# One transformer layer on one core: projections of a group interleaved with attention of the group ahead, transposes by DMA inside SBUF

## The chip, the cores and the metric

The kernel runs on one NeuronCore of one Trainium2 chip. The number that counts is the device time of one execution in microseconds. A core has five engines that run side by side: TensorE (PE in the profile; its weight loads are PEld), VectorE (DVE), ScalarE (ACT), GpSimd (POOL) and SyncE (SP), whose queue here issues every DMA. They meet only at semaphores.

## What is computed

The input x is 4 batches of 2048 rows of 512 numbers in fp32. The reference, cut to what matters:

```python
h = layernorm(x)
q, k, v = relu(h @ Wq + bq), relu(h @ Wk + bk), relu(h @ Wv + bv)
e = q @ k.T / sqrt(512)          # causal: later keys are masked
y = softmax(e) @ v               # per batch
x = x + layernorm(relu(y @ Wo + bo))
h2 = layernorm(x)
# for two scores (so, si): grouped convolution of h2 (4 columns to 1),
# batch norm over all 8192 rows, gelu, linear, softmax
out = (h2 @ W) * top32(softmax(so)) + (h2 * top32(softmax(si))) @ W + bias
x = x + layernorm(out)
```

The batch norm needs the mean and variance over all rows of all batches. So there are two phases: the first (layer norm, attention, residual, the convolution and its statistics) has to end before the second (gelu, linear, top 32, the output) may begin.

## The kernel before

A tile is 128 rows, so a batch has 16 tiles, and a group is 4 tiles (512 rows). Every fp32 operand of a large product is split into two fp16 halves, hi and lo, and `three` (L445 to L450) issues three matmuls for each product: hi by hi, hi by lo, lo by hi. A full step is 4 slices of 128 in the contraction by 3, which is 12 matmuls of 128x512.

The first phase (L342 to L941) is a hardware loop over the 4 batches (`Fori`), one body for each engine. What PE does in the body, in this order, is `pe_steps` (L217 to L231):

- For each of the 4 groups: 4 steps each of v, k and q (a step is 128 of the 512 output channels), in which the tiles of the next group are transposed (`hT`), and then 4 steps `vo`, which multiply v by Wo ahead of the attention. This part of the body is called projections below.
- Then, for i from 0 to 17 (`attention_steps`, L200): the scores of tile i against all keys up to it (`s`, one step for each chunk of 512 keys), and for tile u = i-2 the product of the softmax with v (`pv`), chunk by chunk. Ahead of the product of a chunk stands the transposition of the next (`pT`). In the last i of a batch the first four tiles of the next batch are transposed as well.

A transposition is done by PE. It takes an fp32 tile in SBUF, multiplies it by the identity (L475, L527) into one of two PSUM banks (`T_BANK`), from which ACT takes the hi half (`hi_half`, L563, with the instruction in L567) and DVE the lo half (`lo_half`, L681, with L685). PE may use the bank again when DVE has read it: `take_t` waits on `t_lo` of two transpositions back (L454). The product of a chunk waits on `t_lo` of its own (L535).

Other banks: 4 (`M_BANK`) for projections, scores and the transposed convolution, 2 (`Y_BANK`) for the products. `take_m` (L457) waits until the step four places back has been read out.

ACT reads each v, k, q step twice (L582 into `raw`, L583 into the hi half), DVE subtracts (L708). ACT takes exp (L658), bias and norm work on the attention output follow on ACT (L592, L597), DVE (L721, L727, L729, L734, L736, L743) and POOL (L894 to L910). DVE does the convolution as a product and a reduction, twice for each tile (L750, L753), PE transposes its result (`conv_transposes`, L464, instruction L467), ACT adds the channel bias (L606), DVE takes the statistics (L759). All three steps of a tile lag its attention by some i.

SBUF: one area `work` of 7168 words serves the transposed input, the input itself, the scores and the transposed softmax in turn, because projections and attention don't overlap. SP issues the loads and stores in order; its plain loads of x go to `work`.

The second phase (L948 to L1400) is a loop over groups of 8 tiles, and the change doesn't touch it but for the view of `bn_all` that L1253 reads.

## Time and profile before

| | |
|---|---|
| median of 3 runs | 2333.42 us (2332.57 to 2333.52) |
| profiled execution | 2331.11 us |
| its span | 2329.3 us |
| PE, DVE, ACT, POOL busy | 90%, 69%, 52%, 39% |
| DMA engines, queue of SP | 19.7% of 16 engines |
| granted clock of TensorE | 0.976 on the mean |

The span is what lies between the first and the last instruction that the profiler recorded, the time is that of the whole execution. PE's line in 40 slices shows the two phases: nines and eights up to slice 27 (about 1570 us), a slice with two tenths, and eights beside a DVE and a POOL at nine after it. Matmuls are pipelined: one of 128x512 is shown with 379 ns, but the next one starts earlier than that, so the busy time of PE is more than the time it needs.

### The profile page before, as it was taken

Reading aid. Unit: us, or ns where it says so; the run is one execution under the profiler, and the core shown is the slowest. Engines: PE = TensorE matmul, PEld = TensorE weight load, DVE = VectorE, ACT = ScalarE, POOL = GpSimd, SP = SyncE. Lnnn points to the kernel's source line nnn. Section 1 sums busy time; section 2 is a strip of 40 time slices with the busy share of each in tenths; the row PEclk is TensorE's granted clock in tenths of the full one; section 3 lists DMA queues with packets and bytes.
Section 4 is the critical chain, followed back from the end, with each engine's and each line's share of the span. In section 5 each row is a group of like instructions: output and inputs, shape, how many; then the busy total and the mean of one; then the engine's idle time right before and its main releaser. Section 6 shows DMA issues by size and latency. Waiting matters only on the chain. (4 is left out here: it accounts for less than half of the span.)

```text
span 2329.3 us, 37816 instructions
## 1 busy us (share of the span) xinstructions
PE 2088.6 (90%) x10313; PEld 1019.8 (44%) x10313; DVE 1596.3 (69%) x3574; ACT 1203.9 (52%) x2483; POOL 906.0 (39%) x1127
## 2 busy tenths in 40 slices
PE   5999999999999899999999999964888887888985
PEld 2444454444455444545444445532333333433432
DVE  6544756543665655376655357577999999999994
ACT  4443323444332344333244433234888888888886
POOL 1101212100221200021210022124999999999998
PEclk9999999999999999999999999996999999999998
DMA  4101212100211200021211012122222222222232
GB/s 146 53 10 39 80 48 76 56 26 7 71 64 48 86 30 33 26 77 62 69 49 42 8 55 80 48 89 96 88 89 84 84 86 90 77 88 89 77 96 76
DMA packets 91008, 151.19 MB, mean 65 GB/s; under 512 B 9538, under 2 KB 27074, under 8 KB 90820
## 3 DMA queue, kind: packets, MB, share of 16 engines
q1 hardware_dynamic: 90820, 149.05, 19.7%
q8 instruction: 73, 1.20, 0.2%
q14 instruction: 115, 0.94, 0.2%
HBM read 86.10 MB, written 62.91 MB: 64 GB/s over the span
## 5 line engine op out<-in xcount | busy, mean ns | idle before, releaser
L448 PE MATMUL psum<-work,w_hi 128*128 128x512 f16 x1536 | 457.9, 380 | 7.3 <-DVE w_lo L678 3.7
L448 PE MATMUL psum<-v,work 128*128 128x512 f16 x1632 | 374.4, 379 | 35.2 <-DVE work L685 35.1
L567 ACT ACTIVATE work<-psum 128x512 f16<-128x512 f32 (+2 forms) x228 | 125.3, 551 | 496.9 <-PE psum L527 462.4
L448 PE MATMUL psum<-kT,qT 128*128 128x512 f16 (+3 forms) x1920 | 364.3, 348 | 0.0
L448 PE MATMUL psum<-work,w_lo 128*128 128x512 f16 x768 | 291.6, 380 | 0.0
L685 DVE SCALAR_TENSOR_TENSOR work<-psum,work 128x512 f16<-128x512 f32 (+2 forms) x228 | 144.1, 632 | 181.2 <-ACT work L567 179.2
L448 PEld LDWEIGHTS psum<-kT,qT 128*128 128x128 f16 x1920 | 181.4, 98 | 168.8 <-issue 2.0
L582 ACT ACTIVATE work<-psum,bqkv_s 128x512 f32<-128x512 f32 x192 | 132.1, 688 | 236.4 <-PE psum L448 233.7
L448 PEld LDWEIGHTS psum<-v,work 128*128 128x128 f16 x1632 | 156.7, 98 | 212.3 <-DVE work L685 48.7
L1292 DVE MAX8 c<-cut 128x8 f32<-128x512 f32 x384 | 244.1, 675 | 4.6 <-DVE cut L1288 4.6
L448 PEld LDWEIGHTS psum<-work,w_hi 128*128 128x128 f16 x1536 | 150.2, 98 | 178.5 <-issue 5.2
L908 POOL TENSOR_SCALAR ve<-mv 128x1 f32<-128x1 f32 x66 | 14.6, 221 | 536.8 <-DVE mv L736 536.8
L894 POOL TENSOR_SCALAR ve<-mv 128x1 f32<-128x1 f32 x65 | 15.8, 244 | 488.9 <-DVE mv L729 485.2
L1076 PE MATMUL psum<-fw,xsT 128*128 128x512 f16 x792 | 197.7, 403 | 1.1 <-ACT xsT L1178 1.1
L1076 PE MATMUL psum<-fw,h2T 128*128 128x512 f16 x780 | 179.3, 379 | 0.0
L1288 DVE MATCH_REPLACE8 cut<-c,cut 128x512 f32<-128x512 f32 x256 | 170.7, 673 | 0.0
L448 PE MATMUL psum<-w_hi,vT 128*128 128x512 f16 x512 | 154.9, 379 | 0.0
L904 POOL TENSOR_TENSOR xr<-ob,xr 128x512 f32<-128x512 f32 x66 | 83.5, 1265 | 146.0 <-ACT ob L597 146.0
L708 DVE TENSOR_TENSOR qT<-work,qT 128x512 f16<-128x512 f32 x64 | 44.3, 692 | 115.6 <-ACT qT L583 115.6
L1076 PEld LDWEIGHTS psum<-fw,xsT 128*128 128x128 f16 x792 | 82.1, 104 | 92.2 <-issue 20.5
L448 PEld LDWEIGHTS psum<-work,w_lo 128*128 128x128 f16 x768 | 75.3, 98 | 91.1 <-issue 0.8
L1076 PEld LDWEIGHTS psum<-fw,h2T 128*128 128x128 f16 x780 | 76.5, 98 | 77.9 <-issue 0.5
(140 smaller groups left out, 3880.1 us busy)
## 6 DMA issues: line engine op xcount, KB each, us to landing
work<-x SPq DMA_DIRECT2D x72, 256.0 KB, 3.2
out<-zn SPq DMA_DIRECT2D x70, 256.0 KB, 3.0
h_scratch<-hb SPq DMA_DIRECT2D x68, 256.0 KB, 3.1
x_scratch<-xr SPq DMA_DIRECT2D x66, 256.0 KB, 2.9
x<-x_scratch SPq DMA_DIRECT2D x66, 256.0 KB, 2.8
h<-h_scratch SPq DMA_DIRECT2D x65, 256.0 KB, 3.7
xr<-x SPq DMA_DIRECT2D x64, 256.0 KB, 2.9
xc_scratch<-xcT SPq DMA_DIRECT2D x68, 128.0 KB, 1.7
```

Of the source, the lines that this page charges most:

```text
L448: mm = nc.tensor.matmul(outp, stat(a), mov(c), start=(n == 0 and k == 0), stop=(n == total - 1 and k == 2))
L567: nc.scalar.activation(dst, src, ACT.Copy, scale=scale).then_inc(t_hi.sem, 1)
L582: nc.scalar.activation(raw[:, n % 2, :], bank, ACT.Relu, bias=bias, scale=QKV_DOWN)
L685: nc.vector.scalar_tensor_tensor(dst, src, scale, hi, ALU.mult, ALU.subtract).then_inc(t_lo.sem, 1)
L708: nc.vector.tensor_tensor(dst[:, 1], raw[:, n % 2, :], dst[:, 0], ALU.subtract).then_inc(vkq_lo.sem, 1)
L894: nc.gpsimd.tensor_scalar(ve2[:], m[:, 1:2], EPS * O_GAIN * O_GAIN, None, ALU.add).then_inc(ve2_ok.sem, 1)
L904: nc.gpsimd.tensor_tensor(xr[:, t % 4, :], ob[:, t % 2, :], xr[:, t % 4, :], ALU.add).then_inc(x1_ok.sem, 1)
L908: nc.gpsimd.tensor_scalar(ve3[:], mv3[:, t % 2, 1:2], EPS, None, ALU.add).then_inc(ve3_ok.sem, 1)
L1076: mm = nc.tensor.matmul(outp, stat(a), mov(c), start=(fresh and n == 0 and k == 0), stop=(n == total - 1 and k == 2))
L1288: nc.vector.match_replace(dst, eight, src, 0.0).then_inc(top_ok.sem, 1)
L1292: nc.vector.max(dst, src).then_inc(top_ok.sem, 1)
```

## The change

The first phase is written anew. The second stays, and so does the arithmetic: the same products in the same halves.

- **Order.** The 16 groups of all batches go through one unrolled program (no `Fori` in the first phase). Time is counted in halves H, eight for each group g. PE's list for a half is `pe_items(H)`: two projection steps of group g (v in halves 0 and 1, q in 2 and 3, k in 4 and 5, vo in 6 and 7), and one piece of attention of group g-1 (scores of its tiles 1, 2, 3 in halves 0, 2, 4, products of its tiles 0 to 3 in halves 1, 3, 5, 6) or, in half 7, the scores of tile 0 of g itself. The later work on a tile (bias, norms, residual, convolution) is given out by `due(H, lag)`. After the last group there are 12 more halves without projections.
- **Transpositions.** `hT` and `pT` on PE are gone (L475, L527). ACT and DVE or POOL make the two fp16 halves in SBUF in the natural layout (`hhl`, `phl`), and SP transposes each half with a DMA from SBUF to SBUF (`dma_start_transpose`). The hi half of the input comes from ACT (`hi_h`), its lo half now from POOL (`lo_h`), those of the softmax from ACT (`hi_p`) and DVE (`lo_p`). The two small transpositions of the convolution stay on PE.
- **Banks.** The two banks of transpositions join the others, so `M_BANK` has 6.
- **Buffers.** The shared `work` area is replaced by buffers of their own: input 4 tiles, its halves 4 tiles, transposed input 2 groups, scores 2 tiles (before 3), softmax halves 4 chunks, transposed softmax 4 chunks (before 2). qT holds two groups in place of a batch.
- **Queues.** SP runs through stores, loads and DMA transposes in one order written out by half. A transpose of chunk n waits for its lo half and for the product of chunk n-4.
- **Start.** The identity, the biases and the mask are loaded behind the weights and the first transposes; PE waits for all five of them before its first matmul. The priming of semaphores and of buffers by zeros, which the loop needed, goes.

The core of the diff:

```diff
+def stages(H):
+    g, h = divmod(H, HALF)
+    kind, c = (VQK + ("vo",))[h // 2], 2 * (h % 2)
+    return [(kind, g, c), (kind, g, c + 1)] if g < NG else []
+def s_tile(H):
+    g, h = divmod(H, HALF)
+    if h == 7 and g < NG:
+        return GROUP * g
+    if h in (0, 2, 4) and 0 < g <= NG:
+        return GROUP * (g - 1) + 1 + h // 2
+    return None
+def pv_tile(H):
+    g, h = divmod(H, HALF)
+    if h in (1, 3, 5, 6) and 0 < g <= NG:
+        return GROUP * (g - 1) + (1, 3, 5, 6).index(h)
+    return None
+def due(H, lag):
+    g, h = divmod(H - lag, HALF)
+    if h in (2, 3, 5, 6) and 0 < g <= NG:
+        return GROUP * (g - 1) + (2, 3, 5, 6).index(h)
+    return None
+def pe_items(H):
+    attention = []
+    if s_tile(H) is not None:
+        attention = [("s", s_tile(H), j) for j in range(chunks(s_tile(H)))]
+    if pv_tile(H) is not None:
+        attention = [("pv", pv_tile(H), j) for j in range(chunks(pv_tile(H)))]
+    items = stages(H) + attention if H % HALF < 2 else attention + stages(H)
+    if due(H, 4) is not None:
+        items.append(("x", due(H, 4)))
...
@@ -92,8 +173,7 @@
-        T_BANK = [psum[:, n, :] for n in (0, 1)]
-        M_BANK = [psum[:, n, :] for n in (2, 3, 4, 5)]
+        M_BANK = [psum[:, n, :] for n in range(6)]
         Y_BANK = [psum[:, n, :] for n in (6, 7)]
 
...
@@ -110,19 +190,17 @@
-            qT = sa("qT", [P, 2, C, S], F16)
+            qT = sa("qT", [P, 2, 2, C, 512], F16)
             kT = sa("kT", [P, 2, C, S], F16)
             v = sa("v", [P, 2, TILES, D], F16)
-            work = sa("work", [P, 7168], F32)
-            hT = [work[:, 2048 * n:2048 * (n + 1)].bitcast(F16).rearrange("p (h c n) -> p h c n", h=2, c=C)
-                  for n in (2, 0)]
-            xg = work[:, 2048:4096].rearrange("p (j n) -> p j n", j=GROUP)
-            raw = work[:, 6144:7168].rearrange("p (s n) -> p s n", s=2)
-            sS = [work[:, 2048 * n:2048 * (n + 1)] for n in range(3)]
-            pT = work[:, 6144:7168].bitcast(F16).rearrange("p (s h n) -> p s h n", s=2, h=2)
             vT = sa("vT", [P, 2, C, 512], F16)
+            hT = sa("hT", [P, 2, 2, C, 512], F16)
+            xg = sa("xg", [P, GROUP, D], F32)
+            hhl = sa("hhl", [P, GROUP, 2, D], F16)
+            raw = sa("raw", [P, 2, D], F32)
+            sS = sa("sS", [P, 2, S], F32)
+            phl = sa("phl", [P, 4, 2, 512], F16)
+            pT = sa("pT", [P, 4, 2, 512], F16)
...
@@ -338,109 +358,104 @@
+                def transpose_h(g, j):
+                    need(sp, vqk_ps, vqk_at("k", g - 2, C - 1))
+                    sp.wait_ge(h_lo.sem, h_lo.at(GROUP * g + j))
+                    for a in range(2):
+                        sp.dma_start_transpose(hT[:, g % 2, a, :, P * j:P * (j + 1)], hhl[:, j, a, :]).then_inc(hT_in[j].sem, 16)
+                def transpose_p(T):
+                    for j in range(chunks(T)):
+                        n, w = chunk_at(T, j), width(T, j)
+                        need(sp, pv_ps, n - 4)
+                        sp.wait_ge(p_lo.sem, p_lo.at(n))
+                        for a in range(2):
+                            sp.dma_start_transpose(pT[:, n % 4, a, 0:w].rearrange("p (c n) -> p c n", n=P), phl[:, n % 4, a, 0:w]) \
+                                .then_inc(pT_in[n % 4].sem, 16)
...
+                for H in range(HALVES):
+                    g, h = divmod(H, HALF)
+                    if h == 3 and pv_tile(H) is not None:
+                        transpose_p(GROUP * (g - 1) + 2)
+                    if h == 5 and pv_tile(H) is not None:
+                        transpose_p(GROUP * (g - 1) + 3)
+                    rows_of(H)
+                    if h == 1 and pv_tile(H) is not None:
+                        transpose_p(GROUP * (g - 1) + 1)
+                    if h == 4 and g + 1 < NG:
+                        transpose_h(g + 1, 0)
+                        transpose_h(g + 1, 1)
+                    if h == 5 and g + 2 < NG:
+                        for j in range(GROUP):
+                            load_x(g + 2, j)
+                    if h == 6 and g + 1 < NG:
+                        transpose_h(g + 1, 2)
+                        transpose_h(g + 1, 3)
+                    if h == 7 and g < NG:
+                        transpose_p(GROUP * g)
...
@@ -449,497 +464,467 @@
+                def take_m(item):
+                    n = m_place[item]
+                    if n >= 6:
+                        signal, i = m_freed(m_items[n - 6])
+                        pe.wait_ge(signal.sem, signal.at(i))
+                    return m_bank(item)
...
+                def product(T, j):
+                    n, t = chunk_at(T, j), T % TILES
+                    if j == 0:
+                        pe.wait_ge(vo_lo.sem, vo_lo.at(T))
+                        need(pe, o_ev, T - 2)
+                    pe.wait_ge(pT_in[n % 4].sem, pT_in[n % 4].at(n // 4))
+                    for k in range(width(T, j) // P):
+                        mm = three(Y_BANK[T % 2], GROUP * j + k, t + 1, lambda a: pT[:, n % 4, a, P * k:P * (k + 1)],
+                                   lambda a: v[:, a, GROUP * j + k, :])
+                    mm.then_inc(pv_ps.sem, 1)
...
+                def hi_h(g, j):
+                    act.wait_ge(hn_ok.sem, hn_ok.at(GROUP * g + j))
+                    need(act, hT_in[j], g - 1)
+                    nc.scalar.activation(hhl[:, j, 0, :], xg[:, j, :], ACT.Copy).then_inc(h_hi.sem, 1)
...
+                def hi_p(T, part):
+                    for j in range(chunks(T))[part]:
+                        n, w = chunk_at(T, j), width(T, j)
+                        act.wait_ge(p_ok.sem, p_ok.at(T))
+                        need(act, pT_in[n % 4], n // 4 - 1)
+                        nc.scalar.activation(phl[:, n % 4, 0, 0:w], sS[:, T % 2, 512 * j:512 * j + w], ACT.Copy, scale=P_SCALE) \
+                            .then_inc(p_hi.sem, 1)
...
-                def lo_half(b, step, dst, hi, scale):
-                    dve.wait_ge(t_hi.sem, t_at(t_hi, b, step))
-                    src = t_bank(step)[:, 0:dst.shape[-1]] if len(dst.shape) == 2 else t_bank(step).rearrange("p (c n) -> p c n", c=C)
-                    nc.vector.scalar_tensor_tensor(dst, src, scale, hi, ALU.mult, ALU.subtract).then_inc(t_lo.sem, 1)
...
+                def lo_p(T, part):
+                    for j in range(chunks(T))[part]:
+                        n, w = chunk_at(T, j), width(T, j)
+                        dve.wait_ge(p_hi.sem, p_hi.at(n))
+                        nc.vector.scalar_tensor_tensor(phl[:, n % 4, 1, 0:w], sS[:, T % 2, 512 * j:512 * j + w], P_SCALE,
+                                                       phl[:, n % 4, 0, 0:w], ALU.mult, ALU.subtract).then_inc(p_lo.sem, 1)
...
+                    if h == 0:
+                        if st:
+                            lo_vqk(*st[0])
+                        late(H, (5, conv_stats), (2, residual_stats))
+                        if st:
+                            lo_vqk(*st[1])
+                        if s is not None:
+                            score_rows(s)
+                        late(H, (3, convolution))
+                    elif h == 1:
+                        early = s_tile(H - 1)
+                        for n, part in ((0, first), (1, rest_of)):
+                            if st:
+                                lo_vqk(*st[n])
+                            if early is not None:
+                                lo_p(early, part)
+                        late(H, (3, convolution))
+                        if g + 1 < NG:
+                            ln_stats(g + 1, 2)
+                            ln_stats(g + 1, 3)
+                    elif h == 2:
+                        if s is not None:
+                            score_rows(s)
...
+                def lo_h(g, j):
+                    pool.wait_ge(h_hi.sem, h_hi.at(GROUP * g + j))
+                    nc.gpsimd.tensor_tensor(hhl[:, j, 1, :], xg[:, j, :], hhl[:, j, 0, :], ALU.subtract).then_inc(h_lo.sem, 1)
```

## Rows read from the trace of the kernel before

**Rows 1.** Busy time by stage: stretch, its length, each engine, granted clock, DMA share, GB/s
```profile
27.60:1558.00 1530.40, 1481.43 (x7549) 745.25 (x7550) 877.44 (x1887) 588.40 (x1054) 227.42 (x412) 1.00 0.15 51
1558.00:1583.00 25.00, 2.97 (x13) 1.38 (x11) 18.04 (x37) 6.16 (x15) 7.60 (x14) 0.60 0.32 110
1583.00:2329.30 746.30, 600.05 (x2737) 270.17 (x2737) 684.91 (x1631) 600.69 (x1407) 663.94 (x684) 0.94 0.28 86
```

**Rows 2.** Timeline of PE in the attention of the last batch: start, length, instructions
```profile
1485.41 9.88 PE L448 MATMUL psum<-kT,qT 128*128 128x512 f16 x48
1495.13 0.60 PE L527 MATMUL psum<-idn,work 128*128 128x128 f32 x4
1495.57 2.75 PE L448 MATMUL psum<-v,work 128*128 128x512 f16 x12
1498.16 0.60 PE L527 MATMUL psum<-idn,work 128*128 128x128 f32 x4
1498.60 2.75 PE L448 MATMUL psum<-v,work 128*128 128x512 f16 x12
```

**Rows 3.** Transpositions on PE, groups by shape: count, busy us, mean ns, idle before
```profile
L527 PE MATMUL psum<-idn,work 128*128 128x128 f32 x544 | 86.2, 274 | 10.2 <-DVE work L685 6.7 <-ACT work L658 3.4
L475 PE MATMUL psum<-idn,work 128*128 128x128 f32 x272 | 42.6, 282 | 19.7 <-DVE work L701 16.9 <-DVEq L796 2.8
L467 PE MATMUL psum<-idn,xcs 128*128 128x128 f32 x132 | 25.7, 277 | 9.3 <-ACT xcT L606 9.3
```

**Rows 4.** What PE's weight loads waited for, 27.6 to 1558 us: us, times, longest
```profile
PEld psum L448 <- DVE work L685: 53.0, 38, 2.8
PEld psum L527 <- DVE work L685: 8.7, 8, 1.9
```

**Rows 5.** DMA: the queue of SP (packets, MB, share), two issues (KB, us to landing)
```profile
q1 hardware_dynamic: 90820, 149.05, 19.7%
xc_scratch<-xcT SPq DMA_DIRECT2D x68, 128.0 KB, 1.7
bqkv_s<-bqkv SPq DMA_DIRECT2D x1, 6.0 KB, 1.6
```

**Rows 6.** Timeline of SP: one issue
```profile
1530.12 0.33 SPq L386 DMA_DIRECT2D xc_scratch<-xcT  x1
```

**Rows 7.** Groups by shape of the engines beside PE, first phase: count, busy us, mean ns
```profile
L582 ACT ACTIVATE work<-psum,bqkv_s 128x512 f32<-128x512 f32 x192 | 132.1, 688 | 236.4 <-PE psum L448 233.7 <-DVE w_lo L678 2.0 <-DVE kT L708 0.7
L567 ACT ACTIVATE work<-psum 128x512 f16<-128x512 f32 x180 | 106.9, 596 | 402.7 <-PE psum L527 368.2 <-PE psum L475 34.1
L685 DVE SCALAR_TENSOR_TENSOR work<-psum,work 128x512 f16<-128x512 f32 x180 | 123.8, 688 | 150.6 <-ACT work L567 148.5 <-ACTq L624 1.8
L835 DVE TENSOR_SCALAR_CACHE_REDUCE work<-psum 128x512 f32<-128x512 f32 x96 | 63.8, 690 | 29.9 <-PE psum L448 28.9
L658 ACT ACTIVATE work<-work,nm 128x2048 f32<-128x2048 f32 x4 | 8.0, 1993 | 0.0
L743 DVE TENSOR_SCALAR hb<-xr,mv,rs 128x512 f32<-128x512 f32 x66 | 38.2, 579 | 0.6 <-POOL rs L910 0.6
L750 DVE TENSOR_TENSOR prod<-hb,cw_b 128x512 f32<-128x512 f32 x131 | 90.3, 690 | 6.4
L753 DVE TENSOR_REDUCE xcs<-prod 128x128 f32<-128x512 f32 x131 | 89.9, 686 | 5.2
L904 POOL TENSOR_TENSOR xr<-ob,xr 128x512 f32<-128x512 f32 x66 | 83.5, 1265 | 146.0 <-ACT ob L597 146.0
```

**Rows 8.** Timeline at the start: layer norm's statistics, its scaling, PE's first product
```profile
9.18 0.18 DVE L696 BATCH_NORM_AGGREGATE mv<-st 128x2 f32<-128x6 f32 x1
...
27.60 1.01 PE L448 MATMUL psum<-work,w_hi 128*128 128x512 f16 x2 [3.70 <-DVE w_lo L678]
```

**Rows 9.** Timeline between the phases: last product, last statistics, second phase's first
```profile
1555.13 2.75 PE L448 MATMUL psum<-v,work 128*128 128x512 f16 x12
...
1583.56 3.64 DVE L1253 BATCH_NORM_AGGREGATE bn_mv<-bn_all 128x2 f32<-128x384 f32 x2 [1.99 <-PEq L342]
```

More of the change, by code:

```diff
@@ L81, in sem, with sig @@
             return ctx.enter_context(nc.semaphore(name))
[L83 to L84 removed]
+        def sig(name, step=1):
+            return Count(sem(name), step)
         x1_d = nc.dram_tensor("x1_scratch", [(B + 1) * TILES + GROUP, P, D], F32, kind="Internal").ap()
@@ new lines, in conv_stats, with late @@
+                def conv_stats(T):
+                    for r in range(2):
+                        wait_apart(dve, x_ev, x_ev.at(T))
+                        i = nc.vector.bn_stats(bn_all[:, T, r, :], xcT[:, T % 2, r, :])
+                    i.then_inc(bn_ok.sem, 1)
+                def late(H, *steps):
+                    for lag, step in steps:
+                        if due(H, lag) is not None:
+                            step(due(H, lag))
+                for j in range(GROUP):
+                    ln_stats(0, j)
```

1006 lines of the change are left out of this document (421 added, 585 removed).

## The prediction

> **What bounds the kernel now.** I read the stages first. The span falls into a start (27.6 us), the first phase up to PE's last product (1530.4), a drain (1558 to 1583.6) and the second phase (745.7) [rows 1, 9]. The second phase isn't touched: its DVE and POOL instructions stay, so its 745.7 us go into the sum unchanged. In the first phase PE shows 1481 of 1530 us at full granted clock, DVE 877, ACT 588, POOL 227 [rows 1]; PE is the bound. How much of that is needed, the busy time doesn't tell, since a matmul's shown length overlaps the next. The timeline does: 12 matmuls of 128x512 begin at 1495.57 and what follows them at 1498.16, so one costs 0.216 us of stream; four transpositions begin there and the next product at 1498.60, so one costs 0.11 [rows 2]. The scores of three full chunks and one of 384 take 9.72 us, which leaves 0.162 for a 384 wide one [rows 2]: cost goes by columns.
>
> From the loops, a batch has 768 projection matmuls, 336 of full score chunks, 408 of products: 1512 x 0.216 = 326.6 us. Narrow chunks are 48 each of 384, 256 and 128 columns, 48 x 0.324 = 15.6. Four batches make 1368.6 us. Transpositions of inputs and softmax: 544 + 272, less 16 before the first product, are 800 x 0.11 = 88 us; those of the convolution 126 x 0.11 = 13.9 [rows 3]. 1530.4 - 1368.6 - 88 - 13.9 leaves 60 us in which PE stood still. The waits name them: its weight loads waited 53.0 + 8.7 = 61.7 us for the lo half of a transposition by DVE [rows 4]. So the transpositions cost 88 us of stream and about 60 of waiting.
>
> **The change, part by part.**
>
> Transpositions off PE: minus 88 us, on the path, as PE is the bound. The convolution's stay, 13.9.
>
> The waits: minus 60, and new ones come. What a product now waits for is a longer chain, but it has a longer lead. Chain after a tile's last score matmul: eviction 0.69, maximum about 0.1, exp up to 1.99, hi half about 0.6, lo half 0.69, two DMA transposes [rows 7], taking the durations of the nearest forms; both halves read SBUF now, which I price the same. That is 4.1 us without the DMAs. Shortest lead, tile 1 in a group with one chunk a tile: two projection steps (5.2), a product, the next scores, two more steps, about 13 us. On the way stand, in DVE's order, a convolution (0.58 + 2 x (0.69 + 0.69) = 3.3 us) and the lo half of the next projection step [rows 7]; so some 9 us plus DMAs against 13. In groups of four chunks the lead is over 20 us for tiles 0 to 2; for tile 3 the transposes wait for the products of tile 2 chunk by chunk (four buffers), so the first pair has two chunks' matmuls of 2.6 us each and the two steps between, some 12 us, and then a pair every 2.6 us.
>
> The six banks: a step waits for the one six places back, 6 x 2.6 = 15.6 us at PE's pace, against 0.69 x 2 of ACT behind an exp of 1.99. I cost it at nothing; ACT's own order covers it.
>
> Other engines: DVE loses the input's lo half (64 x 0.688 = 44 us), ACT's count stays, POOL gains 64 x 1.265 = 81 us [rows 7]. DVE 877 - 44 = 833 of some 1410 us, ACT 588, POOL 308: none is a bound on the mean. By group it is closer. One with attention of one-chunk tiles gives PE 41.5 us of projections (192 x 0.216) and 10 blocks of 128x128 keys at 1.3 (12 narrow and 3 wide matmuls): 54 us. DVE has 16 lo halves (11 us), four tiles of later work at about 6.4, input statistics and scaling 6, scores and softmax halves 6: 48 to 49. So DVE is at nine tenths there, in four groups of 16. I put 2 us into each.
>
> The DMA transposes: 128 for inputs and 320 for softmax chunks. Counted in blocks of 128x128 that is 512 + 1088 = 1600, so 400 full ones of 128x512 fp16 (128 KB). They go through one queue in order. PE leaves 1412 / 400 = 3.5 us for each. In a group with four-chunk tiles there are 148 blocks, 37 full ones, in 41.5 + 58 x 1.3 = 117 us: 3.2 us each. The trace has no such DMA. From below: a plain one of 128 KB is issued in 0.33 us and lands after 1.7 [rows 5, 6]. From above: the queue's 90820 packets took 19.7% of 16 engines over 2329.3 us, which is 81 ns each at 1.6 KB [rows 5]. A transpose can't move rows of 1 KB whole. Cut at the 128 columns of a block it has 512 packets, 512 / 16 x 81 ns = 2.6 us; cut into half that, 5.2 us, and finer still 10. A packet of little content should cost less than 81 ns: the bias load, 128 runs of 48 bytes, lands in 1.6 us like the large one [rows 5]. I take 2.2 us, between 1.7 and 2.6, the ends nearest to a row. At 2.2 the queue is used for 880 of 1412 us and the transposes are hidden, but the tight leads above (9 us plus a pair of 4.4 us against 13) are used up. I put 30 us of stalls into the sum (0 to 60): 8 for DVE, 12 for eight groups with short tiles at 1.5 us, 10 for the fourth tiles and the last group, whose attention no projections cover.
>
> Here two rules of the Trainium skill stand against each other, and the trace can't decide. "Advanced Engine Details and Errata", section on the X-bar transpose, says that transpose DMAs on this chip are as fast as regular ones: then the sum holds with stalls near 0. "VectorE: DVE Perf Modes", section on the three transpose paths, lists 1309 ns for a 128x128 block by DMA. Taken as time for each of four blocks one after the other, that is an estimate of 5.2 us for a full one, and the kernel would take about 2890 us.
>
> Start: statistics end at 9.18 before [rows 8]; then scaling, hi halves, POOL's four lo halves (5.1 us), eight transposes behind 4 MB of weights, and five constants behind those, for which PE now waits. I get 27 to 34 us for the first product, and take 30 (27.6 before).
>
> Drain: from the last product the last tile goes through bias, relu, statistics, scale, norm, residual, statistics, norm, two convolutions, a transposition and statistics: about 13 us of instructions and 17 hand-overs of 0.15, the tile before it adds a convolution on DVE: 22 us to the second phase (25.6 before) [rows 9].
>
> Sum: 30 + 1368.6 + 13.9 + 30 + 22 + 745.7 = 2210.2 of span. The profiled execution took 1.8 us more than its span, and the median of the runs is 2.3 above that execution: 2214 us.
>
> **The rivals.** (a) The queue isn't full, but the chain comes late. SP works in one order; behind a transpose that waits for a product stand the next group's input transposes, the loads and the stores of finished tiles. At 3 us for a transpose a pair takes 6, a tile of four chunks 24, and the fourth tile's last pair arrives some 2 to 3 us late, in each of 32 tiles with three or four chunks; with DVE's tight groups that makes 80 more us: about 2290 (2240 to 2325). For it: PE's present waits show that any late half stops it at once. Against: leads of 12 us and more.
>
> (b) The transposes are the bound. From 3.5 us for a full one on, the first phase lasts 400 times that; at 3.8 nothing is gained, at 4.0 the time is 30 + 1600 + 22 + 745.7 + 4 = 2402, at 4.6 about 2640, at 5.2 about 2880. PE would show long waits for DMA, and its granted clock would fall below the 1.00 of rows 1. For it: packets of half a block's row give 5.2. Against: the short runs of the bias load, and an average use of the queue of only 19.7% now. The rule of the 1309 ns is this rival's.
>
> (c) The change brings nothing: idle time moves from the transpositions' lo halves to other steps of an order written by hand, 115 us of it, through DVE. DVE has 833 us of work in 1530, so this needs it to block in every half: unlikely.
>
> **How the numbers follow.** Forecast 2214, its own range 2185 to 2245: chance 0.50. (a) 0.19. (b) 0.24. (c) 0.03 for within 0.2%. The rest, 0.04, is faster than 2185 (start at 27, drain 18, no stalls give 2175). What this measurement can tell from no change is about 0.2%, 5 us. Faster: 0.50 + 0.19 + 0.04 = 0.73; same 0.03; slower 0.24. The range is 2185 to 2400: it takes in (a) and the part of (b) up to 4.0 us for a transpose, and leaves out 0.04 below and some 0.15 above.
>
> **What would show it.** Right: in the stretch from the first to the last product PE's stream holds only 128x512 products and the convolution's transpositions, its waits add up to 10 to 60 us, a DMA transpose of 128 KB lands 2 to 4 us after its issue, SP is occupied for under two thirds of the first phase, and the last product ends near 1440 us. Wrong: waits of PE's products for DMA into pT of several us each, every group (a or b); a time between issues of transposes near 3.5 us or more, whatever stands between them (b); the second phase's length off 746 by more than 5 us; a first product after 40 us.

## Result: the changed kernel and its profile

The changed kernel takes **2181.72 us** (median of 4 runs, 2180.44 to 2182.61) against 2332.99 for the kernel before beside it (2330.07 to 2333.52): a ratio of 0.9353, 95% interval 0.9338 to 0.9368, or 151 us less. Forecast were 2214 us and 2185 to 2400, so the side and the likeliest mechanism were right, and the time lies 3 us below the range. The profiled execution took 2180.44 us, its span is 2178.7.

The stages (start of the first phase's products to their end, drain, second phase; columns as in [rows 1]):

```profile
29.90:1418.20 1388.30, 1384.04 (x6746) 655.51 (x6747) 826.67 (x1788) 576.15 (x1041) 306.77 (x464) 1.00 0.38 91
1418.20:1437.40 19.20, 1.76 (x8) 0.78 (x6) 11.67 (x26) 4.42 (x11) 6.25 (x11) 0.63 0.26 96
1437.40:2178.70 741.30, 598.61 (x2737) 270.58 (x2737) 685.32 (x1631) 601.36 (x1407) 663.46 (x684) 0.94 0.28 86
```

The first phase's stretch fell from 1530.4 to 1388.3 us. The stream of products (1368.6) and of the convolution's transpositions (13.9) makes 1382.5 of it, so only 5.8 us are left in which PE stood still, where the same sum on [rows 1] left 60. DVE is busy for 827 us (forecast 833), ACT 576, POOL 307 (308). Groups by shape of the other engines, in the first of these stretches, answer to [rows 7]:

```profile
L564 ACT ACTIVATE raw<-psum,bqkv_s 128x512 f32<-128x512 f32 x192 | 131.4, 685 | 241.6 <-PE psum L463 240.6
...
L719 DVE SCALAR_TENSOR_TENSOR phl<-sS,phl 128x512 f16<-128x512 f32 x112 | 72.5, 679 | 3.7 <-ACT phl L584 3.7
L886 POOL TENSOR_TENSOR hhl<-xg,hhl 128x512 f16<-128x512 f32 x60 | 69.8, 1197 | 6.5 <-ACT hhl L554 6.5
L704 DVE TENSOR_SCALAR_CACHE_REDUCE sS<-psum 128x512 f32<-128x512 f32 x96 | 66.2, 691 | 134.7 <-PE psum L463 134.2 <-issue 0.4
L584 ACT ACTIVATE phl<-sS 128x512 f16<-128x512 f32 x112 | 65.5, 625 | 0.1
```

The softmax halves read SBUF now and cost about what they did from PSUM: 679 ns on DVE for 688, 625 on ACT for 596. POOL's lo half of the input takes 1197 where 1265 was assumed. The ends of these stages come from the timelines of PE and DVE:

```profile
29.93 1.03 PE L463 MATMUL psum<-hT,w_hi 128*128 128x512 f16 x2 [29.93 <-DMA cw_b<-convw]
```
```profile
1397.94 20.26 PE L463 MATMUL psum<-v,pT 128*128 128x512 f16 x93
```
```profile
1437.40 1.89 DVE L1238 BATCH_NORM_AGGREGATE bn_mv<-bn_all 128x2 f32<-128x384 f32 x1 [2.05 <-PEq L365]
```

The end of the chain is visible here as well: the last 93 products run without a gap, where [rows 2] had a transposition and a hand-over between every twelve. The waits of PE's matmuls (us, times, longest) that the transposes cause are these, against [rows 4]:

```profile
PE psum L463 <- DMA cw_b<-convw: 29.9, 1, 29.9
PE psum L463 <- DMA pT<-phl: 4.2, 3, 1.7
```

What a DMA transpose costs stands in the answers on its two lines in the program (SP's issue in ns, minimum, median and maximum, and the time to landing), in SP's timeline, and in the queue's row, against [rows 5, 6]:

```profile
L388 SPq DMA_TRANSPOSE pT<-phl x320: 1127/1232/2292, 73.2 to 1411.9; - x160
DMA to landing us min/median/max: 2.2/2.5/4.5
```
```profile
L379 SPq DMA_TRANSPOSE hT<-hhl x128: 1199/1263/2782, 10.1 to 1231.9; - x128
```
```profile
1312.79 8.26 SPq L388 DMA_TRANSPOSE pT<-phl x6
1351.15 10.30 SPq L388 DMA_TRANSPOSE pT<-phl x8
```
```profile
q1 hardware_dynamic: 308036, 198.13, 34.7%
```

Eight transposes in 10.30 us are one every 1.29 us, and SP's issue of 1.23 is nearly all of it (other runs of eight took 10.35 and 11.08). The landing is counted from the start of the issue, so at 2.5 us about two overlap. The DMA engines aren't full meanwhile: in 11 us of such transposes back to back the queue's packets took under half of the 16 engines.

```profile
q1 hardware_dynamic: 4096, 0.98, 47.2%
```

That is the queue's row for the stretch from 1384 to 1395 us, 4096 packets for 8 transposes, 512 for each. The first pair of the program, whose chunks are only 128 wide, takes SP 1.2 us each as well:

```profile
73.22 2.41 SPq L388 DMA_TRANSPOSE pT<-phl  x2
```

So SP's cost goes by instruction, not by blocks. The queue's packets grew by 217,216, their time from 0.197 x 2329.3 x 16 to 0.347 x 2178.7 x 16 us, which is 22 ns for each added packet, not the 81 of a packet of 1.6 KB.

The three waits for pT stand at 461, 808 and 1155 us, once in each batch after the first, always at the fourth tile of a group whose tiles have one chunk. The first of them, in SP's timeline and PE's:

```profile
452.75 5.12 SPq L379 DMA_TRANSPOSE hT<-hhl  x4
457.96 2.52 SPq L388 DMA_TRANSPOSE pT<-phl  x2
```
```profile
461.88 2.75 PE L463 MATMUL psum<-v,pT 128*128 128x512 f16 x12 [1.28 <-DMA pT<-phl]
```

The lo half of this chunk was ready at 457.0 us (DVE's L719, 456.30 and 0.71 long), but in SP's order its pair of transposes stands behind four of the next group's input. This place decides what a dearer transpose costs (experiment 7).

**Where the 150.6 us of span went** (2329.3 less 2178.7): 88 of stream (worked out from [rows 2, 3], not measured alone), 54 of waits (60 less 5.8, what remains of the two stretches when the streams are taken off), 6.4 in the drain (25.6 less 19.2), 4.4 in the second phase, less 2.3 for the later start.

### The profile page after: what moved, and what is told of

Its sections match the earlier page's. It is cut to its first block and busy times, and to the rows that moved or that the text cites. A ratio compares the mean times of both kernels' runs of the same rounds, so it can differ in the third digit from the quotient of the medians.

```text
span 2178.7 us, 33778 instructions
## 1 busy us (share of the span) xinstructions
PE 1984.4 (91%) x9489; PEld 926.9 (43%) x9489; DVE 1540.1 (71%) x3461; ACT 1193.0 (55%) x2468; POOL 985.9 (45%) x1176
## 5 line engine op out<-in xcount | busy, mean ns | idle before, releaser
L463 PE MATMUL psum<-hT,w_hi 128*128 128x512 f16 x1536 | 458.4, 380 | 29.9 <-DMA cw_b<-convw 29.9
L463 PE MATMUL psum<-v,pT 128*128 128x512 f16 x1632 | 362.5, 379 | 4.2 <-DMA pT<-phl 4.2
L463 PE MATMUL psum<-hT,w_lo 128*128 128x512 f16 x768 | 291.8, 380 | 0.0
L564 ACT ACTIVATE raw<-psum,bqkv_s 128x512 f32<-128x512 f32 x192 | 131.4, 685 | 241.6 <-PE psum L463 240.6
L463 PEld LDWEIGHTS psum<-v,pT 128*128 128x128 f16 x1632 | 159.4, 98 | 194.0 <-issue 5.6
L463 PEld LDWEIGHTS psum<-hT,w_hi 128*128 128x128 f16 x1536 | 150.5, 98 | 203.9 <-DMA cw_b<-convw 29.9
L575 ACT ACTIVATE sS<-sS,nm 128x128 f32<-128x128 f32 (+7 forms) x64 | 76.9, 1201 | 290.0 <-DVE nm L711 290.0
L704 DVE TENSOR_SCALAR_CACHE_REDUCE sS<-psum 128x512 f32<-128x512 f32 x96 | 66.2, 691 | 134.7 <-PE psum L463 134.2
L691 DVE SCALAR_TENSOR_TENSOR v<-psum,v 128x512 f16<-128x512 f32 x64 | 44.0, 688 | 105.1 <-ACT v L570 105.1
L686 DVE TENSOR_TENSOR qT<-raw,qT 128x512 f16<-128x512 f32 x64 | 44.1, 689 | 105.0 <-ACT qT L565 104.9
```

What stands on the lines that cost most here:

```text
L463: mm = nc.tensor.matmul(outp, stat(a), mov(c), start=(n == 0 and k == 0), stop=(n == total - 1 and k == 2))
L564: nc.scalar.activation(raw[:, n % 2, :], bank, ACT.Relu, bias=bias, scale=QKV_DOWN)
L575: nc.scalar.activation(sS[:, T % 2, 0:w], sS[:, T % 2, 0:w], ACT.Exp, bias=nm[:, T % 3:T % 3 + 1], accum_out=ssum[:, T % 3:T % 3 + 1]).the ...
L704: nc.vector.tensor_scalar(dst, src, S_SCALE, None, ALU.mult, ALU.max, accum_out=pm[:, T % 3, j:j + 1]).then_inc(s_ev.sem, 1)
```

## Experiments

All were compared with the kernel before on the same chip, which stood at 2332.2 to 2333.8 us beside each set of runs. "Stopped or slowed" below is the time from PE's first product to the second phase's first statistic, less 1401.7 us (1382.5 of stream and 19.2 of drain); it is 5.8 for the changed kernel. "Gaps" are the stretches between the first and the last product in which the trace shows no matmul: 49.0 us for the kernel before, 4.2 for the changed one. They are less than what the sums call stops, because a lone matmul is shown longer (379 ns) than its stream (216), and because some time is lost at the lower of the two levels of the granted clock (1.2 and 2.4 GHz).

**1. The loop written out, and nothing else.** Kernel before, first phase unrolled (`b_unroll`).

```diff
-                with pe.Fori(0, B) as b:
+                for b in range(B):
...
-    nc = bacc.Bacc("TRN2", target_bir_lowering=False, num_devices=1)
+    nc = bacc.Bacc("TRN2", target_bir_lowering=False, num_devices=1, dynamic_dma_scratch_size=1024)
```

Expected: 

> The kernel before with its first phase written out four times in place of the hardware loop, and with the small reserved scratch of the new kernel (1024), which moves all buffers in SBUF; order and transpositions as before. Theory A: the first phase keeps its 1530 us; time 2333 us, less at most 4 us if the second phase's 745.7 us become the new kernel's 741.3 through the place of its buffers. Theory C (writing out the loop is a part of the gain: no loop ends, no addresses from registers): first phase under 1515 us, time under 2318.

Measured: 2326.82 us (2324.73 to 2330.08), ratio 0.9973 [0.9964, 0.9983], against 2333.78 beside it. In the trace, first product at 28.11, last end 1557.4: 1529.3 us where the loop took 1530.4, so theory A holds for the first phase. Another 2.6 lie in the second phase (743.1 against 745.7). By the medians, writing out the loop and moving the buffers are worth 6 to 7 us together, somewhat more than theory A allowed; the profiled executions show 3.0 of them. The second phase's 4.4 us of the change may have the same root in part.

**2. The new order alone, transpositions kept on PE.** In the changed kernel, the transpositions return to PE as pieces set between the projection steps, with two banks of their own (four left for the rest).

```diff
+    st = stages(H)
+    mixed = st[0:1] + t_items(H, 0) + st[1:2] + t_items(H, 1)
+    items = mixed + attention if H % HALF < 2 else attention + mixed
...
+        T_BANK = [psum[:, n, :] for n in (4, 5)]
```

Expected: 

> The new order by halves is kept, with everything unrolled, but inputs and softmax are transposed by PE again (fp32, two PSUM banks, so four for the rest), each piece placed behind a projection step one half ahead of its use. Theory A (the gain has two parts: 88 us of PE's stream by taking transpositions off it, and some 55 us of waits by the longer lead of the new order): only the 88 us come back, with waits of PE for lo halves of 0 to 20 us in place of 62; about 2268 us (2255 to 2290). Theory B (the DMA transposes are the whole gain; interleaving with PE's transpositions still stops PE at each lo half): 2320 to 2335.

Measured: 2325.14 us (2321.34 to 2326.69), ratio 0.9966 [0.9953, 0.9978], theory B's figure. Against the changed kernel this is the way of transposing alone, in the same order (and with four banks for six, which experiment 4 prices at 3 us or less): 143 of the 151 us go when the transpositions leave PE, though this version's first product comes 11 us earlier than the changed kernel's. First product at 18.45, last product's end 1559.5: 1541.0 us, less 1470.5 of stream (1382.5 and 88) is 70 us of stops, no fewer than the 60 before, though a projection step stands on either side. The gaps are 49.1 us, as before the change; another 11 were lost at the lower level of the granted clock, where the kernel before loses 2. The 8 us by which this version is faster lie outside the stretch, in an earlier start (9), the drain (6) and the second phase (4), less the 11 that the stretch is longer. Its waits, matmuls and then weight loads from 18 or 40 us to 1560:

```profile
PE psum L469 <- DVE pT L723: 31.9, 27, 3.3
PE psum L536 <- DVE pT L723: 15.6, 14, 4.1
```
```profile
PEld psum L469 <- issue: 56.5, 77, 3.8
PEld psum L536 <- DVE pT L723: 30.5, 36, 4.3
```

Where the trace names a releaser, it is DVE's late half still, as in [rows 4]; 56.5 us of the weight loads' idle time have none. Setting the pieces ahead of the projection steps in place of behind them (`mixed = t_items(H, 0) + st[0:1] + t_items(H, 1) + st[1:2]`, the halves on ACT and DVE likewise) was the second try at this order:

Expected: 

> As the kernel with PE's transpositions in the new order, but each pair of pieces stands ahead of a projection step and not behind it, so that at least one step (2.6 us) covers the two halves. Theory A' (with enough lead PE's transpositions cost only their stream): 2182 + 88 = 2270 us and up to 20 of waits, 2265 to 2290. Theory B (whatever the order, PE stops at lo halves behind DVE's other work, and its clock falls after the stops; only transposes off the engines end that): 2305 or more.

Measured: 2331.24 us (2326.99 to 2334.02), ratio 0.9989 [0.9979, 0.9999]. It is 6 us worse, with 79 us of stops by the same sum (gaps 56.4, lower clock 14), and again theory B's figure. In the two placements tried, the interleaving gives nothing while the transposition goes through one of two PSUM banks and its evictions. That no placement could isn't shown.

**3. Stream off PE in the old order.** Kernel of experiment 1, with one transposition of 128x128 for each bank in place of up to four (it leaves the other blocks untransposed).

```diff
-                    for c in range(C):
+                    for c in range(few):
...
-                            for n in range(min(GROUP, u + 1 - GROUP * g)):
+                            for n in range(1):
```

Expected: 

> The kernel before, its batch loop written out (that alone: 2326.8 us), with one transposition of 128x128 on TensorE in place of up to four for each bank, inside the first phase: 576 fewer of 0.11 us, 63 us less of TensorE's stream; evictions, halves and order stay (it leaves out three quarters of the transpositions' work). Theory A (stream time and waits are independent terms, as the forecast summed them): 2260-2268 us. Rival B (the halves' chain on ACT and DVE, 1.3 us, is then covered by less stream, so waits grow): 2270-2300, with TensorE's waits for DVE's lo half above the 62 us of the kernel before. Rival C (waits take nearly all of it): above 2300.

Measured: 2276.08 us (2275.65 to 2276.7), ratio 0.9757 [0.9741, 0.9774]; 50.7 us below experiment 1 for 63.4 us of stream. The products run from 27.29 to 1507.3 us, 1480 for a stream of 1407, so stops grew from 59 to 73: with less stream beside it, the same chain of halves is less hidden. Rival B is met in its time. Its sign was waits for DVE's lo halves above 62 us, and the weight loads show 52. But the version it was made from has 42, so these waits did grow, by 10 of the 14 us.

**4. The banks.** `M_BANK` of 4 in place of 6 in the changed kernel.

```diff
-        M_BANK = [psum[:, n, :] for n in range(6)]
+        M_BANK = [psum[:, n, :] for n in range(4)]
```

Expected: 

> The changed kernel with four banks for projections, scores and convolution in place of six. Theory A (four steps of 2.6 us cover ACT's 3.4): 2178 to 2190, no change that can be told. Rival (the two banks that the transpositions gave back carry a part of the gain: ACT's exp and the softmax halves stand ahead of a read-out): 2200 or more, waits of PE for ACT.

Measured: 2184.83 us (2183.4 to 2188.58), ratio 0.936 [0.9345, 0.9376]. Theory A is met. Its first product came at 31.46, 1.5 us later than the changed kernel's, so the two freed banks are worth 3 us at most, and experiment 2 wasn't slow for having only four banks for projections and scores. Whether its two banks for transpositions were too few wasn't tried.

**5. The lead of a softmax chunk.** Two buffers each for `phl` and `pT` in place of four.

```diff
+RING = 2
-            pT = sa("pT", [P, 4, 2, 512], F16)
+            pT = sa("pT", [P, RING, 2, 512], F16)
...
-                        need(sp, pv_ps, n - 4)
+                        need(sp, pv_ps, n - RING)
```

Expected: 

> The changed kernel with two buffers in place of four for the softmax halves and for their transposes. A transpose of a tile's third chunk then waits for the product of its first, and SP stands in order before it. Theory A (the lead is what hides a transpose; without it each costs issue and landing): third and fourth chunks late by 1 to 5 us each in 32 tiles, more by the order of SP: 2300 to 2450. Rival (the queue is quick enough without a lead): under 2230.

Measured: 2258.45 us (2256.01 to 2262.91), ratio 0.968 [0.9661, 0.9698]: 77 us given back, between the two expectations. In its waits PE stops for the DMA 44 times:

```profile
PE psum L464 <- DMA pT<-phl: 60.3, 44, 2.7
```

Half of what the change gains needs the two further buffers: 2.6 us of stream for a chunk are less than the pair of transposes (2 x 1.29 and a landing). 83 us are stopped or slowed and PE's gaps are 66.2 us, more than the 60 and 49.0 with PE's transpositions. So leaving PE and its banks doesn't by itself end the waits; it takes the lead that four buffers allow.

**6. Plain copies in place of the transposes.** The same 448 DMAs, sizes and order, without the transposition, which is left out.

```diff
-                            sp.dma_start_transpose(pT[:, n % 4, a, 0:w].rearrange("p (c n) -> p c n", n=P), phl[:, n % 4, a, 0:w]) \
+                            sp.dma_start(pT[:, n % 4, a, 0:w], phl[:, n % 4, a, 0:w]) \
```

Expected for one execution: 

> Each DMA transpose replaced by a plain copy of the same 128 KB within SBUF, so attention and projections work on data that isn't transposed; the timing is that of the same program. Both theories: 2175 to 2185, as the transposes are hidden. A plain copy should take SP 0.4 us in place of 1.25 and land after 1.7 to 2.0 us in place of 2.5, by the rows of 128 KB stores.

And for several: 

> The kernel after with plain copies in place of the 448 DMA transposes (it leaves the transposition out), timed in rounds as the base for the next two; one execution took 2176.2 us. Both theories of those: 2174-2178 us.

Measured: 2176.24, and 2174.91 us (2172.46 to 2176.19), ratio 0.9322 [0.9306, 0.9337]. The answer on the line, to set beside that of the transpose:

```profile
L388 SPq DMA_DIRECT2D pT<-phl x320: 464/547/1735, 71.8 to 1402.2; - x160
DMA to landing us min/median/max: 1.7/2.0/4.2
```

A plain copy of this shape is issued in 0.55 us and lands in 2.0; a transpose takes 0.68 us more of SP and 0.5 more to land. (For the inputs, whose copy was written with a split destination, it is the other way round in the landing: 3.5 us for the copy, 2.6 for the transpose.) PE doesn't wait for any of them; the stops are 1.0 us. So real transposes cost this kernel 7 us against plain copies: 2.8 by the later first product (29.9 for 27.2), 4.8 in stops.

**7. What a dearer transpose does.** This is the test of the forecast's price. First the real transposes, with one and with two more of 128x128 into a spare tile behind each:

```diff
+                        sp.dma_start_transpose(dum[:, m % 2, :], w_hi[:, 0, 0, 0:P]).then_inc(spare[m % 2].sem, 16)
```

Expected of one more: 

> The changed kernel with one more DMA transpose (128x128, into a buffer nobody reads) behind each of its 448 (none for group 0's input). SP then issues about 1066 us of transposes and 150 of other DMAs in 1388. Theory A (stalls are small because a transpose costs SP 1.25 us and the queue has room): the time stays within 20 us, 2183 to 2200; in tiles of four chunks a pair takes about 4.8 us instead of 2.4, so only the fourth tiles run late, by about 1 us each. Theory D (the forecast's leads were right and tight, 30 us of stalls at 2.2 us for a transpose): 2210 or more.

Expected of two more: 

> Two more DMA transposes (128x128) behind each. SP then needs 448 x 1.25 + 880 x 1.15 + 150 us = 1720 us, more than PE's 1388. If SP's issue is what a transpose costs, the first phase ends about 1750 us and the kernel takes about 2510 us (2450 to 2560). If transposes issued back to back overlap and the queue isn't a bound: under 2300.

Measured: 2303.08 us (2300.35 to 2303.67), ratio 0.9871 [0.9854, 0.9887], and 2775.3 in one execution. The first is far above theory A's 2183 to 2200. The second is above even the 2450 to 2560 of a queue that is simply full. To go finer, and to tell SP's time from the traffic of transposes, one, two, two or three in turn, and three small plain copies were put ahead of each operand's copy in the kernel of experiment 6 (at the start, one store also waits for the weights' halves, which these copies read):

```diff
+                def extra():
+                    for _ in range(3):
...
+                        sp.dma_start(dum[:, m % 8, :], w_hi[:, 0, 0, 0:32]).then_inc(spare[m % 8].sem, 16)
```

Expected of three: 

> The plain-copy version (it leaves the transposition out) with three more small copies of 128x32 ahead of each operand's copy, from the second group on for the inputs, so that SP is occupied about 2.1 us for each instead of 0.55 to 0.65 (the kernel after: 1.25), near the 2.2 us on which the forecast rested, and each operand lands some 1.5 us later. Theory A (the forecast's law: 30 us of stalls at this price): 2200-2215 us. Theory D (the leads are used up sooner, as the doubled version, at 2.5 us, took 2303): 2225-2290 us, with TensorE waiting 40 us or more for DMA into pT and a granted clock below 1.00 in the windows with the stops. Under 2190 would say that it was not SP's time but the transposes' own traffic that made the doubled version slow.

Expected of one: 

> The plain-copy version (it leaves the transposition out) with one small copy ahead of each operand's: SP occupied about 1.25 us for each, as in the kernel after. Theory A (the 6.8 us between the plain-copy version, 2174.9, and the kernel after, 2181.7, are SP's time and the later landing): 2178-2185. Rival B (they are the transposes' own traffic of small packets or the later constants at the start): 2174-2177.

Expected of two: 

> The same with two small copies ahead: SP occupied about 1.9 us for each operand. Theory A (a knee: nothing is lost until SP's time for the 28 operands of a full group nears what TensorE leaves, then all of it is): 2185-2205. Theory D (loss grows evenly between 0.6 us and 2.5 us, 80 us per us): 2265-2285. Between them, 2205-2265, a curve that bends upward.

Expected of two and three in turn: 

> The same with two and three small copies in turn: SP occupied about 2.2 us for each operand, the price that the forecast took. Theory A (the forecast's law, 30 us of stalls): 2200-2215. Theory D (the even curve): 2290-2300. By a straight line between the two neighbours: their middle.

Measured (ratios 0.9965 [0.9951, 0.9979], 0.9341 [0.9326, 0.9357], 0.9476 [0.946, 0.9491], 0.9627 [0.9611, 0.9643] in that order). The period is the time from one operand's issue to the next in SP's timeline, back to back:

| version | period, us | first product | second phase | stopped or slowed | of it PE's matmuls waiting for DMA (the gaps) | time, us |
|---|---|---|---|---|---|---|
| plain copies | 0.6 | 27.2 | 1429.8 | 1.0 | 0 | 2174.9 |
| one more | 1.3 | 27.3 | 1435.6 | 6.6 | 4.9 | 2179.4 |
| **the changed kernel** | 1.29 | 29.9 | 1437.4 | 5.8 | 4.2 | 2181.7 |
| two more | 1.93 | 27.9 | 1465.7 | 36.1 | 26.3 | 2210.7 |
| two or three | 2.25 | 27.8 | 1501.9 | 72.4 | 56.0 | 2245.7 |
| three more | 2.57 | 27.7 | 1581.1 | 151.7 | 107.2 | 2325.9 |
| transpose doubled | 2.58 | 30.4 | 1557.4 | 125.3 | 85.5 | 2303.1 |
| transpose tripled | 3.86 | 32.1 | 2031.3 | 597.5 | 440.4 | 2775.3 |

Three rows of SP's timeline, with two more, show how such a period is read (from 400.81, where an operand is issued, to 402.74, where the next is, with two small copies between):

```profile
400.81 0.60 SPq L401 DMA_DIRECT2D pT<-phl  x1
401.52 1.18 SPq L378 DMA_DIRECT2D dum<-w_hi  x2
402.74 0.60 SPq L401 DMA_DIRECT2D pT<-phl  x1
```

Plain copies with the changed kernel's period give its stops (6.6 and 5.8), so it is SP's time that counts, and not the packets. The loss bends upward: 47 us for each us of period between 1.3 and 1.93 (29.5 / 0.63), 113 between 1.93 and 2.25, 248 between 2.25 and 2.57. Of the expectations, those of one more (theory A) and of two more (a curve that bends upward) are met; 2.25 us fits none of its three, and three more took longer than either theory's figure. At 2.25, the period nearest to the price that the forecast took, the kernel takes 2246 us, and 72 us are stopped or slowed instead of the 30 it was given.

Where the time goes can be read from the places of the gaps. At 1.93 us, 21 of the 26.3 us lie in the groups with one-chunk tiles, and the other 5 in the last group, which no projections cover. At 2.25 these are 32 and 13 of 56; only 11 lie in all other groups together, though SP has more to issue in those. The longest gap of each batch is the one seen above at 461.88, at the fourth tile, behind four input transposes. Here it is with two more copies:

```profile
470.96 3.57 PE L477 MATMUL psum<-v,pT 128*128 128x512 f16 x8 [5.62 <-DMA pT<-phl]
```

Six operands stand in a row there, four of the input and the tile's own pair, so 0.64 us more for each should make it about 3.8 us longer; it went from 1.3 to 5.6.

The two columns of lost time differ, more so the longer the stops. Most of the missing part is clock. With three more copies, 151.7 us are 107 of gaps, 37 that PE's matmuls lost at the lower level of the granted clock (half the time in which PE was busy there), and some 8 left over; 39 stops at 0.16 us, the difference between a matmul's shown length and its stream, would make 6 of these. At 2.25 us the clock's part is 11 of 72. In the windows of the version with three more copies it falls where PE had stopped:

```profile
1380.00:1400.00 20.00, 20.00 (x99) 9.46 (x97) 11.42 (x22) 7.44 (x13) 0.00 (x0) 1.00 0.34 88
...
1480.00:1500.00 20.00, 15.44 (x65) 6.64 (x64) 8.25 (x15) 2.66 (x6) 0.00 (x0) 0.91 0.34 85
...
1540.00:1560.00 20.00, 12.90 (x41) 4.57 (x42) 9.95 (x17) 0.63 (x1) 3.24 (x7) 0.74 0.31 75
```

and 24 products take longer behind a stop than in a run of work (same kernel, PE's timeline):

```profile
1439.67 5.34 PE L477 MATMUL psum<-v,pT 128*128 128x512 f16 x24
...
1543.70 7.83 PE L477 MATMUL psum<-v,pT 128*128 128x512 f16 x24 [4.77 <-DMA pT<-phl]
```

A stop of 4.77 us was followed by a loss of another 2.5 us (7.83 against 5.34); in the trace the granted clock stands at the lower level, 1.2 GHz, from 1541.4 to 1548.2 us.

**8. The start.** In the kernel of experiment 6, PE, ACT and DVE wait for the five constants only where they use them.

```diff
-                pe.wait_ge(const_in, 16 * 5)
...
                 def conv_transposes(T):
                     bank = take_m(("x", T))
+                    pe.wait_ge(const_in, 16 * 5)
```

Expected: 

> The plain-copy version (it leaves the transposition out), but TensorE, ScalarE and VectorE do not wait for the five constants at the start, only where they use them. In the plain-copy version the first product starts at 27.97 us, behind a wait for the last constant. Theory A (only the constants hold it): first product at 23.5-26 us and the end 2 to 4.5 us earlier than the plain-copy version beside it. Rival B (the inputs' copies land no earlier): first product at 27 us or later, no change beyond 1 us.

Measured: 2170.59 us (2170.21 to 2172.57), ratio 0.9304 [0.9288, 0.9319], 4.3 below 2174.91. The first product waits for the inputs now:

```profile
23.81 1.01 PE L463 MATMUL psum<-hT,w_hi 128*128 128x512 f16 x2 [23.81 <-DMA hT<-hhl]
```

That is 3.3 us earlier, of which 2.5 are left at the start of the second phase (1427.4 for 1429.8). With the real transposes it wasn't measured. There SP issues the first eight until 23.2 us, so by adding their landing of 2.6 an estimate is 26 against 29.9; a kernel of 2178 us should be within reach, but none of the runs here shows it.

## Why the prediction was right or wrong

**Bound and stream: right.** PE sets the first phase, and its needed work, counted by stream and not by busy time, came out within 5.8 us: 1388.3 measured for 1382.5 worked out. With plain copies only 1.0 is left over (experiment 6), so the count by columns holds to a tenth of a per cent.

**The waits that go: right in size, and the cause is narrower than "the change".** 60 became 5.8. Experiments 1 and 2 show that neither the unrolling nor the interleaving removes them: with transpositions on PE they are 59, 70 or 79 in three orders. What removes them is the way by DMA together with four buffers of lead; with two buffers as many come back (experiment 5). How much of it is the absent bank and eviction, and how much the longer lead, isn't separated. Whether the old order with DMA transposes would reach the same time wasn't tried; experiment 3 shows only that in it 63 us less of stream give 51. The interleaving may be needed for the leads.

**The price of a transpose: wrong, and this is the step that failed.** The text said: "I take 2.2 us, between 1.7 and 2.6", and from it "I put 30 us of stalls into the sum (0 to 60)". A transpose takes 1.29 us of the queue in order, and the stalls are 5.8 us. The price was worked out from packets, 512 at 81 ns over 16 engines. The number of packets was right for a full chunk (4096 for eight transposes), the time of one was not: 22 ns. The nearest row for a small packet was there, the bias load [rows 5], and was used as an argument but not as a value. It was also the wrong resource: SP's issue sets the pace at 1.23 us, a cost for each instruction. No row of the kernel before gave its size; the nearest was 0.33 us for a plain store [rows 6]. Of the 30, the 8 for DVE in the one-chunk groups had nothing behind them: with plain copies 1.0 us is lost in the whole phase. The rule of the Trainium skill that transposes are as fast as regular DMAs ("Advanced Engine Details and Errata", section on the X-bar transpose) comes close for the landing, 2.5 against 2.0 us (and 2.6 against 3.5 for the inputs), but not for SP, 1.23 against 0.55. The 1309 ns that the Trainium skill lists for a block of 128x128 by DMA ("VectorE: DVE Perf Modes", the three transpose paths) are met only if they are taken as the time of one instruction: a transpose of four blocks has a period of 1.29 us. Rival (b), which took them four times, falls.

**The stalls at a price: wrong the other way.** The forecast had 30 us of stalls at 2.2 and 110 at 3.0. Measured are 36 at 1.93, 72 at 2.25 and 152 at 2.57. Two reasons show in the traces. The short tiles' groups lose the most (32 of 56 us of gaps at 2.25), because their fourth tile waits in SP's order behind four input transposes; the forecast named this order for rival (a) only, and put 12 us on eight groups of short tiles. And a stop costs more than its length by the granted clock (11 us at 2.25), which the forecast named for rival (b) only. The two mistakes had opposite signs, and that the likeliest time came within 32 us is luck to that extent. Along the measured curve the price was worth 66 us too much (72.4 at 2.25 less 5.8 at 1.29), the law gave 42 too little at that price (30 for 72.4), and 24 are left.

**Start, drain, second phase.** Forecast 30, 22 and 745.7; measured 29.9, 19.2 and 741.3. The start's cause was named rightly: PE waits for the five constants, and experiment 8 shows, for plain copies, that nothing else holds it before 23.8 us. The drain was 2.8 shorter. The second phase was taken as unchanged and was 4.4 shorter: DVE is busy there for 685.3 us after 684.9, so it isn't shorter work, and where the idle time went stays open. In experiment 1, 2.6 of it came with the unrolled first phase alone.

**The sum by its terms:** 2210.2 was forecast for the span, 2178.7 measured. Of the 31.5 between them 24.2 are the stalls (30 less 5.8), 2.8 the drain, 4.4 the second phase, 0.1 the start. The profiled execution then lay 1.3 us below the median, where 2.3 was carried over. With the measured stalls alone the forecast would have been 2190; that the time is below 2185 took the drain and the second phase as well.

**The rivals.** (a) 2290, the chain late: it exists from about 1.9 us on, and is dearer than that rival said: 125 to 152 us stopped or slowed at 2.57 (experiment 7), where it had 110 at 3. And it comes first in the short tiles' groups and in the last one, not in the fourth tiles of four chunks. (b) fell with the price. (c), that idle time moves elsewhere, is what happens when the transpositions stay on PE (experiment 2), and not for the change as made. "0.04 faster than 2185" was too little: the range's low end was the sum without stalls, with no room for a drain and a second phase that each end a few us early. The forecast's own corner for this case adds up to 2177 by its terms, not 2175; the measured time lies above it. Of its signs, the stops (5.8 for 10 to 60) and the last product's end (1418.2 for about 1440) were off on the good side; the landing (2.5), SP's share (51% of the stretch) and the second phase (within 5 us) came as said.

## What to carry over

Price a DMA on the path by what issues it as well as by what moves it: at 1.3 us of an in-order queue each, transposes by DMA are hidden here behind a TensorE that gives 2.6 us for a chunk, and at 1.9 no longer. Look for the shortest lead with the longest row of other issues ahead of it in that queue; the stops begin there and not where the queue is busiest. A transposition that leaves TensorE can free more than its stream (54 us of waits here beside 88), if buffers enough give it a lead; interleaving it in the two ways tried does not. And when a term's price is uncertain, ask the nearest row for each resource it uses, work out the sum at that row, and let the range reach it.

## What the runs showed that was not expected

- A DMA transpose inside SBUF of 128 partitions by 128 to 512 fp16 costs SP 1.2 to 1.3 us in the median, nearly without regard to width, and lands in 2.5 us; its packets take 22 ns each of an engine on the mean.
- SP issues a plain DMA from SBUF to SBUF, 8 KB or 128 KB, in 0.55 to 0.65 us in the median, but a store to DRAM in 0.33 [rows 6] (0.33 to 0.58 in the changed kernel).
- At 2.25 us for an operand SP's queue isn't full in any group under projections (40 operands, 90 us, in the 117 us of the fullest), and 72 us are lost already. Half of the gaps among them (28 of 56) stand where one pair of transposes waits behind four others. A queue in order doesn't have to be full to stop its reader.
- In three of the windows of 20 us that hold stops of 1 to 5 us the mean granted clock was 0.74 to 0.91, and 24 products took 7.83 us in place of 5.34.
